# One pair of segment-sum matmuls behind each of thirty tiles of a step, in place of pieces of four to eight

## The reference, cut to what matters

```python
h = jnp.maximum(_layernorm(x), 0.0)
# layer 0
H = h @ W.T + b                                   # then a batch norm over the nodes
msg = H[src] * (dinv[src] * dinv[dst])[:, None]
out = jax.ops.segment_sum(msg, dst, num_segments=n)
x = x + relu(out + H * (dinv * dinv)[:, None])
# layer 1
h = jnp.maximum(_layernorm(x), 0.0)
agg = jax.ops.segment_sum(edge_attr, edge_dst, num_segments=n)
model_in = jnp.concatenate([h, agg, u[batch]], axis=1)
x = x + (relu(relu(model_in @ W1 + b1) @ W2 + b2) @ W3 + b3)
```

## Time and profile before

| | |
|---|---|
| median of three executions | 1194.56 us |
| profiled execution, its time | 1195.33 us |
| its span, first to last instruction | 1193.6 us |
| mean granted clock of TensorE | 0.909 |
| TensorE matmul busy | 1013.2 us, 85% |
| TensorE weight load busy | 682.4 us, 57% |
| VectorE busy | 586.6 us, 49% |
| ScalarE busy | 499.0 us, 42% |
| GpSimd busy | 585.2 us, 49% |
| DMA, mean of the 16 engines | 129 GB/s over the span |

### The profile page before, as it was taken

How to read it: one execution, slowest core, us unless ns; L and a number is a source line. 1 busy time by engine, 2 the same in 40 slices (tenths; PEclk the granted TensorE clock), 3 DMA queues, 4 the chain that set the end, 5 groups by cost and what they waited for, 6 DMA issues and landing times. The chain is left out here.

```text
span 1193.6 us, 23689 instructions
## 1 busy us (share of the span) xinstructions
PE 1013.2 (85%) x9255; PEld 682.4 (57%) x9255; DVE 586.6 (49%) x1338; ACT 499.0 (42%) x894; POOL 585.2 (49%) x574
## 2 busy tenths in 40 slices
PE   3875599889888898888898988888988889999888
PEld 2654266556555565555565765555655556557645
DVE  7988264435443444444443644343544344443375
ACT  3255264334443334333444534343443344443376
POOL 4124604665555565556564165556555556550324
PEclk9787689999988998988998998899989999889889
DMA  6004433545454444444454445454535444451403
GB/s 163 3 2 139 148 130 119 168 131 166 123 165 127 143 152 151 137 150 144 127 166 123 137 129 166 126 160 139 163 123 163 131 136 157 123 165 55 121 1 108
DMA packets 87064, 154.65 MB, mean 130 GB/s; under 512 B 10966, under 2 KB 36884, under 8 KB 87004
## 3 DMA queue, kind: packets, MB, share of 16 engines
q1 hardware_dynamic: 71004, 121.11, 31.4%
q0 software_dynamic: 16000, 32.80, 9.8%
HBM read 147.46 MB, written 6.41 MB: 129 GB/s over the span
## 5 line engine op out<-in xcount | busy, mean ns | idle before, releaser
L968 POOL DMA_INDIRECT gathered<-scaled_h_table,index x500 | 519.1, 1038 | 456.9 <-PE ps_sums L1203 299.7
L980 ACT CAST counts_sb<-ps_counts 128x588 f16<-128x588 f32 x560 | 383.2, 690 | 591.7 <-PE ps_counts L1159 441.5
L1165 PE MATMUL ps_product<-counts_sb,table_sb 128*128 128x240 f16 x2744 | 474.8, 279 | 18.2 <-issue 17.8
L1159 PE MATMUL ps_counts<-key_hot,lo_hot 128*128 128x294 bf16 x1120 | 349.6, 317 | 64.4 <-ACT counts_sb L980 34.0
L1165 PEld LDWEIGHTS ps_product<-counts_sb,table_sb 128*128 128x128 f16 x2744 | 277.3, 102 | 83.5 <-issue 27.7
L1189 PE MATMUL ps_sums<-attr,attr_hot 128*32 128x128 f32 x2240 | 193.0, 287 | 44.4 <-issue 37.6
L1100 DVE TENSOR_TENSOR acc<-acc,ps_product 128x96 f32 (+1 forms) x137 | 37.4, 273 | 390.2 <-remote 216.8
L1042 DVE TENSOR_TENSOR key_hot<-key,iota_key 128x1176 bf16<-128x1176 f16 x280 | 214.0, 764 | 0.0
L1159 PEld LDWEIGHTS ps_counts<-key_hot,lo_hot 128*128 128x128 bf16 x1120 | 114.5, 104 | 145.3 <-ACT counts_sb L980 57.5
L1189 PEld LDWEIGHTS ps_sums<-attr,attr_hot 128*32 128x32 f32 x2240 | 111.1, 111 | 109.8 <-issue 108.5
L1037 DVE TENSOR_TENSOR lo_hot<-src_lo,iota_key 128x512 bf16<-128x512 f16 x280 | 119.0, 425 | 76.8 <-PE ps_counts L1159 75.0
(11 more groups left out here) (228 smaller groups left out, 713.7 us busy)
## 6 DMA issues: line engine op xcount, KB each, us to landing
attr<-in_edge_attr_dram SPq DMA_DIRECT2D x80, 1280.0 KB
gathered<-scaled_h_table,index POOLq DMA_INDIRECT x500
acc<-in_x_dram SPq DMA_DIRECT2D x4, 768.0 KB, 8.8
scaled_h_table<-table_sb SPq DMA_DIRECT2D x12, 256.0 KB, 2.3
xs<-in_x_dram SPq DMA_DIRECT2D x12, 256.0 KB, 5.2
out_dram<-y_ring SPq DMA_DIRECT2D x12, 256.0 KB, 2.3
attr<-in_edge_attr_dram SPq DMA_DIRECT2D x2, 320.0 KB
attr<-in_edge_attr_dram SPq DMA_DIRECT2D x1, 640.0 KB
```

The lines of the kernel that those rows point to most:

```text
L968: pool.indirect_dma_start(gathered[:, n % GATHERS, g, :], None, table, bass.IndirectOffsetOnAxis(ap=index[:, s * CG + g, t:t + 1], axis=0) ...
L980: act.copy(counts_sb[s % 2][:, :, 2 * k * WT:(2 * k + 2) * WT] .rearrange("p h (t n) -> p t h n", n=WT), ps_counts[n % 2][:, :, 0:KEYS].re ...
L1159: pe.matmul(ps_counts[pair % 2][:, c, 0:KEYS], lo_hot[:, b, part, :, c], key_hot[:, b, part, :, c], start=True, stop=True).then_inc(built, 1)
L1165: ins = pe.matmul(ps_product[side][:, 0:SLOTS], table_sb[:, h, low, :], counts_sb[side][:, h, :], start=(part == 0), stop=(part == 2 * NB ...
```

## The change: what it does

The same matmuls are done in the same order within a chunk, in other places. The call moves into the loop over the two tiles of a pair, so `SUMS` is now indexed by the tile q and not by the pair p.

- Attributes: 30 places a step with one sub-tile and two groups, which is 2 matmuls. Chunk 0 stands behind q = 2 to 11, chunk 1 behind 15 to 24, chunk 2 behind 28 to 37.
- Rows: 10 places with one sub-tile and two groups, which is 4 matmuls, behind q = 12, 13, 14, 18, 25, 26, 27, 32, 38 and 39. At 18 and 32 they follow an attribute pair directly.
- `save_sums` on ScalarE moves from pairs 5, 11 and 17 to 6, 12 and 19.
- `sum_rows` waits once for each sub-tile and signals `rows_used` behind the second half.

```diff
+        FIRST, SECOND = range(0, CG // 2), range(CG // 2, CG)
+        SUMS = {first + k * GT + t: [(j, groups, t)] for j, first in enumerate((2, 15, 28))
+                for k, groups in enumerate((FIRST, SECOND)) for t in range(GT)}
+        for n, q in enumerate((12, 13, 14, 18, 25, 26, 27, 32, 38, 39)):
+            SUMS[q] = SUMS.get(q, []) + [(3, (FIRST, SECOND)[n % 2], n // 2)]
...
-                                    if p == 5:
+                                    if p == 6:
                                         save_sums(ATTR_NO[s, 0])
-                                    if p == 11:
+                                    if p == 12:
                                         save_sums(ATTR_NO[s, 1])
-                                    if p == 17 and gathers(s):
+                                    if p == 19 and gathers(s):
                                         save_sums(ATTR_NO[s, 2])
...
-                            def sum_rows(k, t, first):
-                                if t == 0:
+                            def sum_rows(k, groups, t, first):
+                                if t == 0 and groups[0] == 0:
...
-                                pe.wait_ge(gather_in[t], k * (16 * CG) + 16 * CG)
+                                if groups[0] == 0:
+                                    pe.wait_ge(gather_in[t], k * (16 * CG) + 16 * CG)
                                 for part in range(2):
-                                    for g in range(CG):
+                                    for g in groups:
...
-                                ins.then_inc(rows_used, 1)
+                                if groups[-1] == CG - 1:
+                                    ins.then_inc(rows_used, 1)
...
-                                    for what, groups, t in (SUMS if gathers(like) else FEWER_SUMS).get(p, ()):
+                                        for what, groups, t in (SUMS if gathers(like) else FEWER_SUMS).get(q, ()):
```

More of the change, by code:

```diff
@@ L828, in gnn_kernel @@
         PART = [range(2 * NB * j // TILES, 2 * NB * (j + 1) // TILES) for j in range(TILES)]
[L832 to L842, removed]
+        FIRST, SECOND = range(0, CG // 2), range(CG // 2, CG)
[3 more added lines that the diff above has]
+            SUMS[q] = SUMS.get(q, []) + [(3, (FIRST, SECOND)[n % 2], n // 2)]
+        FEWER_SUMS = {q: [piece for piece in pieces if piece[0] < 2] for q, pieces in SUMS.items()}
         def gathers(s):
@@ L1260, in step @@
                                             multiply(side, PART[TILES - LAG + q])
-                                    for what, groups, t in (SUMS if gathers(like) else FEWER_SUMS).get(p, ()):
[L1262 to L1268, removed]
+                                        for what, groups, t in (SUMS if gathers(like) else FEWER_SUMS).get(q, ()):
+                                            if what < 3:
+                                                a_like = ATTR_NO[like, what]
+                                                loads = i * 48 - (like + odd) * 24 + 16 * (a_like // 2 + 1)
+                                                sum_attr(s, k, a0 + what, a_like % 2, loads, what, groups, t, first)
+                                            else:
+                                                sum_rows(k, groups, t, gathered_before(like) == 0)
                                     if p == 3 and old:
```

## The result

| | before | after |
|---|---|---|
| median of 18 runs each | 1194.04 us (1191.11 to 1196.91) | 1190.68 us (1186.41 to 1193.65) |
| profiled execution: time / span | 1195.33 / 1193.6 us | 1189.86 / 1188.1 us |
| mean granted clock | 0.909 | 0.968 |
| TensorE matmul busy | 85% | 90% |

The ratio is 0.9974, with a 95% interval of 0.9963 to 0.9985: faster by 0.26%, which is all but level, where 1280 us was forecast. A cost and a gain of some 140 us each stand behind that number, and they nearly cancel.

The account below looks back on a forecast made before the run. TensorE was taken to bound the edge pass. Per step 3.8 for added work, less 1.1 for the clock, plus 0.5 for handovers made 3.2 us, +85 us in all on 1195.3: 1280 us, range 1180 to 1350.

Parts of the forecast that it names:

- What bounds the kernel: Edge pass: TensorE sets the pace, 36.25 us a step, of which 28.5 us are work and placing.
- W: TensorE's undisturbed work and placing in one step of the edge pass: 28.5 us before, 33.7 after the change.
- neither: The 7.7 us of a step beyond W: 2.3 from the slow clock, 5.4 from holes while gathers run.
- Attribute pairs and rows: TensorE's added places: 18 more for attributes cost 4.0 us a step, halved rows 1.2 more.
- rival of the cheap switch: TensorE's added places cost only 0.10 us each and the clock comes back: 1195 to 1225 us, chance 0.10.
- Handovers: TensorE's next chunk waits for ScalarE's copy of the previous sums: 0 to 1.0 us a step, 0.5 taken.
- Clock: More even TensorE work may remove the deep hole that slows the clock: 0 to 2.3 us back, 1.1 taken.
- The slowed stretches: Beside the step's 20 gathers TensorE runs at 0.58 pace for 12.8 us; added work costs 3.8 us a step.
- Evens out: Some 5.7 of the 7.7 us a step come back, so level within 0.2%: 1192 to 1197 us, chance 0.04.
- even work with two matmuls at a time: Rival: short attribute pieces remove TensorE's holes and keep the clock full, 34.2 us a step: 1149 us, chance 0.17.
- The likeliest case: Main case for the whole kernel: slower, 1225 to 1320 us, likeliest 1280, chance 0.44.
- The signs: If right: 0.44 us per attribute pair, transposes 39 to 40 us apart, slow clock in most steps, PE share falling or level.

Follow-up runs that it names:

- e16: Kernel before, but rows in ten halves behind tiles 10 to 13, 24, 25 and 34 to 37; high level: 1291.92 us, ratio 1.0722.
- e6: Kernel before, but rows in ten halves behind tiles 10 to 13, 24, 25 and 34 to 37; low level: 1025.82 us, ratio 1.0411.
- e13: Kernel before, but its whole rows pieces stand behind tiles 13, 18, 26, 32 and 39; high level: 1123.20 us, ratio 0.9360.
- e10: Kernel before, but its whole rows pieces stand behind tiles 13, 18, 26, 32 and 39; low level: 981.88 us, ratio 0.9974.
- e9: The changed kernel itself, run again beside the kernel before; low level: 1124.46 us, ratio 1.1431.
- e14: Kernel before with each gather replaced by a plain transfer of 64 KB on the same queue; high level: 983.73 us, ratio 0.8195.
- e8: Kernel before with each gather replaced by a plain transfer of 64 KB on the same queue; low level: 985.09 us, ratio 1.0003.
- e18: Kernel before, but whole rows pieces crowded behind tiles 12 to 16, so all five buffers are given back together; high level: 1548.48 us, ratio 1.2857.
- e3: Kernel before with only the attributes changed, to thirty pairs; rows whole behind tiles 11, 13, 25, 35 and 37; high level: 1289.90 us, ratio 1.0805.
- e5: Kernel before, but its whole rows pieces stand behind tiles 13, 18, 26, 32 and 39; low level: 982.30 us, ratio 0.9970.

## Why the prediction was wrong

What each kernel loses, as its time at the high level less its time at the low one, over 25 steps:

| rows | high | low | lost a step | of it in a full step of the loop | runs of gathers in most full steps, high |
|---|---|---|---|---|---|
| before | 1194.0 | 984.0 | 8.4 | 8.1 (36.26 - 28.15) | 8, 8, 4 |
| halves, crowded (e16, e6) | 1291.9 | 1025.8 | 10.6 | 10.6 (40.31 - 29.75) | 8, 8, 4 |
| whole, spaced (e13, e10) | 1123.2 | 981.9 | 5.7 | 5.2 (33.22 - 28.06) | five of 4 |
| after (e9) | 1190.7 | 1124.5 | 2.6 | 2.2 (35.46 - 33.27) | five of 4 |
| plain transfers (e14, e8) | 983.7 | 985.1 | 0 | 0 (28.15 - 28.15) | none (plain ones: 8, 8, 4) |

The column before the last is from the traces, by the starts of each step's first build; for before at the low level it has e8's 28.15, the same order on TensorE. About half of the rest is step 0, which takes 35 to 40 us at the high level in every kernel with gathers, and 21 at the low level and in e14 (27 in e9).

A full step of e18 has one run of twenty and takes 51.0 us, 23 more than the 28.06 of the whole, spaced rows (it wasn't run at the low level). So the loss goes with the length of the runs, and not with it alone: before and e16 have the same runs and lose 8.1 and 10.6; after and e13 both have fours and differ by a factor of two; steps of after have 5 us more of other work beside the same twenty gathers, but that wasn't tried alone. Nor does one run at the high level change the length of the runs and leave TensorE's order as it is. That the places of the rows decide the loss is shown (e13, e16, e18); that they do so through the length of the runs is argued, from the lateness that grows inside e18's run, and from the order of the losses with runs of four, eight and twenty.

Point by point, by the prediction's steps:

- *What bounds the kernel.* Right. W was put at 28.5 us, and the low level shows it bare, 28.15. The 7.7 us that were "neither" are the loss beside the gathers, 8.1 in the full steps.
- *Attribute pairs and rows.* Right. A pair between tiles was put at 0.44 us (0.22 for two matmuls, 0.22 for the place) and takes 0.44. A half of rows, 0.33, takes 0.31. W of after less W of before was put at 5.2 us a step and is 5.1 (e9). The change's own price, 5.2 times 25 and 5 for the steps without a gathered chunk, was 135 us; e9 shows 140.5. The split holds too: the pairs' 4.0 is 4.1 or 4.2, and the rows' 1.2 is 0.9, since the two halves behind an attribute pair, put at 0.11 each, cost nothing. (The 1.68 a step of e6 is for five places that all stand alone.) The rival of the cheap switch falls.
- *Handovers.* 0 to 1.0 us, 0.5 taken. At the low level none is left beyond the 5.1. At the high level the two holes ahead of tiles 2 and 28 end with copies of counts, not with those of sums. So this term was about nothing.
- *Clock.* I gave half back, 1.1 us a step. It came back whole: 1.00 from 400 to 1000 us of the span. It came back with the long hole, so it belongs to the next point.
- *The slowed stretches.* This is the step that failed. "Gathers stay 20 a step, 25 us of issue" took the number of gathers for their effect, and held 12.8 us of slowed stretches fixed, at one pace of 0.58. The number did stay, at nearly the same duration (1023 ns in the mean, 1038 before). But what the same twenty gathers cost depends on where the rows stand (e13, e18), by all signs mostly because that sets how many come unbroken, and the halves' new places moved the moments at which buffers are given back. The loss went from 8.1 to 2.2 us in a full step, where the prediction left 5.2 of it (its step of 39.4 less 0.5 for handovers and less its W of 33.7). Of the 3.9 us between its 39.4 and the 35.46, 1.8 are slowed stretches (4.0 left against 2.2), 1.2 the clock, 0.5 the handovers and 0.4 W (33.7 against 33.27). The prediction has the row that would have led there, GpSimd's idle time before each gather, but listed only two gathers of one run, and of the diff's effect on `rows_used` it said nothing. Each sub-tile's buffer is freed at q = 13, 18, 26, 32 and 39 where it was 11, 13, 25, 35 and 37: gaps of 5, 8, 6 and 7 tiles in place of 2, 12, 10 and 2.
- *The rivals.* "Evens out", 1192 to 1197 us with a chance of 0.04, is where it nearly fell, by luck: 5.9 of 8.1 us came back against 5.1 added. But its mechanism, even work with two matmuls at a time, is refuted by e3. The likeliest case, 1225 to 1320, has no match either: the high level gave 1191, and at the low one, where nothing is lost beside gathers, the change is 14% slower (e9).
- *The signs.* Of those for being right only the 0.44 us of a pair came. The transposes are 35.46 us apart and not 39 to 40, the clock is 1.00 in the loop, and TensorE's busy share rose from 85% to 90%.

## What to carry to other kernels

When a change moves the instruction that gives a buffer back, write down the times at which the refilling engine will start again, before pricing anything else: five releases moved by one to five tiles each were worth 6.4% (e13), and crowded together they cost 29% (e18), twice what all the matmul places of this change cost (14%, e9). A stretch that is slow "while" another engine works need not be a fixed tax by count; measure whether it grows with the length of the burst, and break the burst up without touching the rest. And if one half of a change has the work and the other the rhythm, run them apart (e13 keeps the gain of 0.936 without the price of 5.1 us a step).

## What the runs showed of the hardware

- The same kernel took 984 us at some times and 1193 to 1204 us at others. Chips with the same number gave both (number 10: 983.97 and 1200.48; number 1: 984.01 and 1204.14), so I can't say whether it is another machine or another time. The duration of a gather is the same at both (1038 ns in the mean in before at the high level, 1033 in e5 at the low one). The difference lies in how late TensorE's completions reach the other engines beside them, and it vanishes with plain transfers. What makes the difference stays open.
- At the high level, the loss of a full step by the unbroken runs of its twenty gathers: fours 2.2 to 5.2 us (after, e13), two eights and a four 8.1 to 10.6 (before, e16), one twenty about 23 (e18). At the low level e5 has twenties and loses nothing.
- A tuning order can flip by level: the changed kernel is 0.3% faster at the high level and 14.3% slower at the low one; e13's order is the best of those tried at both (0.936 and 0.997).
- On TensorE a change between full-width and 32-column matmuls costs 0.22 us there and back together, for pieces of 2, 4 or 6 f32 matmuls alike (e8 and e9). Two kinds of 32-column matmuls, one directly behind the other, pay it once: four f16 ones cost 0.31 us alone and nothing behind a pair of f32 ones (e9).
